# Mixture of experts: dense experts replaced by 23 blocks of 128 gathered rows, weights of all experts on chip

## The reference

```
logits = xt @ router_w.T + router_b            # 8 routed experts
top_vals, top_idx = top_k(softmax(logits), 2)
top_vals = top_vals / sum(top_vals)
h = einsum('td,efd->tef', xt, w_up)            # 256 -> 512
y = einsum('tef,edf->ted', silu(h), w_down)    # 512 -> 256
out = einsum('ted,te->td', y, combine)         # combine is 0 except for two experts
out = out + silu(xt @ shared_w_up.T) @ shared_w_down.T
x = x + out
```

## Time and profile before

| what | value |
|---|---|
| median of 3 runs | 2829.75 us (2828.48 to 2829.79) |
| span of the profiled execution, first to last instruction | 2820.9 us |
| TensorE busy in the span | 2592.8 us (92%) |
| VectorE, ScalarE, GpSimd busy | 1386.3, 1042.5, 532.0 us |
| granted TensorE clock, mean | 0.967 |
| mixture layer, first instruction to the first of the next layer | 998.75 to 1267.14 us |

### The profile page before, as it was taken

The page is one execution under the profiler, slowest core; times in us unless marked ns, Lnnn a source line. Parts: engine busy times, 40 slices in busy tenths (PEclk is TensorE's granted clock), DMA queues, the critical chain, the costliest instruction groups (busy, mean ns, idle before and its releaser), DMA issues. The chain is left out here.

```text
span 2820.9 us, 91874 instructions
## 1 busy us (share of the span) xinstructions
PE 2592.8 (92%) x42047; PEld 1855.1 (66%) x42047; DVE 1386.3 (49%) x2238; ACT 1042.5 (37%) x1400; POOL 532.0 (19%) x400
## 2 busy tenths in 40 slices
PE   7999999999999789998999999999979999988798
PEld 3666666666666556664666666666647777777466
DVE  4454544544544831115545455555465454554378
ACT  2333333333323421114444444444434445444223
POOL 2423424434324000002111111111011111111000
PEclk8999999999998579999999999999999999999899
DMA  2110110110100030101111111112010000000200
GB/s 90 32 43 25 37 37 25 37 37 27 42 20 2 1 121 30 45 20 44 43 33 41 34 40 37 37 37 68 3 51 3 3 3 3 4 3 4 79 1 16
DMA packets 49607, 88.88 MB, mean 32 GB/s; under 512 B 8544, under 2 KB 44224, under 8 KB 47952
## 3 DMA queue, kind: packets, MB, share of 16 engines
q1 hardware_dynamic: 49200, 83.08, 9.6%
q0 software_dynamic: 32, 0.02, 0.0%
HBM read 82.04 MB, written 1.05 MB: 29 GB/s over the span
## 5 line engine op out<-in xcount | busy, mean ns | idle before, releaser
L634 DVE TENSOR_REDUCE x_mx<-banks 128x2 f32<-128x800 f32 (+1 forms) x512 | 505.3, 990 | 162.4 <-PE banks L779 133.2
L804 PE MATMUL banks<-x_wv,x_cT 128*128 128x256 f32 (+1 forms) x1664 | 419.3, 394 | 12.3 <-DVE x_nmb L641 12.3
L709 PE MATMUL banks<-x_cT,x_wk 128*128 128x400 f32 (+1 forms) x1024 | 385.4, 519 | 9.3 <-DMA x_cT<-in_ctx 5.9
L804 PEld LDWEIGHTS banks<-x_wv,x_cT 128*128 128x128 f32 (+1 forms) x1664 | 296.4, 187 | 83.6 <-issue 24.5
L527 ACT ACTIVATE x_PT<-banks 128x2048 f32<-128x2048 f32 (+1 forms) x112 | 196.5, 1755 | 372.1 <-PE banks L839 372.1
L529 ACT ACTIVATE x_PT<-banks,x_kbs 128x1024 f32<-128x1024 f32 (+1 forms) x208 | 221.1, 1110 | 287.7 <-PE banks L839 287.7
L652 DVE COPY x_V<-banks 128x512 f32<-128x512 f32 (+1 forms) x224 | 146.2, 653 | 338.1 <-PE banks L804 337.7
L709 PEld LDWEIGHTS banks<-x_cT,x_wk 128*128 128x128 f32 x1024 | 189.5, 193 | 140.5 <-issue 26.8
L839 PE MATMUL banks<-x_qbd,x_kT 32*128 32x128 f32 x6656 | 248.6, 272 | 0.0
L839 PEld LDWEIGHTS banks<-x_qbd,x_kT 32*128 32x128 f32 x6656 | 244.0, 183 | 3.5
L821 PE MATMUL banks<-x_PT,x_V 128*32 128x64 f32 x13312 | 233.8, 221 | 3.8 <-issue 3.0
(11 more groups left out here) (353 smaller groups left out, 3671.4 us busy)
## 6 DMA issues: line engine op xcount, KB each, us to landing
x_cT<-in_ctx SPq DMA_DIRECT2D x96, 400.0 KB, 3.6
x_cT<-in_ctx SPq DMA_DIRECT2D x32, 401.0 KB, 3.6
e_wu<-in_mo_up SPq DMA_DIRECT2D x9, 512.0 KB, 3.5
e_wd<-in_mo_down SPq DMA_DIRECT2D x9, 512.0 KB, 4.5
x_mrow<-in_mask_row SPq DMA_DIRECT2D x1, 3202.0 KB, 16.2
t_w<-in_db_w SPq DMA_DIRECT2D x3, 1024.0 KB, 7.2
d_wqk<-in_db_qk SPq DMA_DIRECT2D x1, 2048.0 KB, 7.9
t_wgu<-in_fp_gu SPq DMA_DIRECT2D x1, 1536.0 KB, 10.4
```

The source lines that it names most:

```text
L634: dve.reduce_max(mx[:, H0[k]:H0[k] + 3:2, kb], g.PS[:, first:first + 2, 0:KBS[kb]], AXX).then_inc(max_read, 1)
L709: last = pe.matmul(PJ[pb][:, 0:KBS[k]], wk[:, c, gg, :], cT[:, (p + 1) % 2, c, KB0[k]:KB0[k] + KBS[k]], start=c == 0, stop=c == KC - 1)
L804: last = pe.matmul(PJ[pb][0:CHK[c + k], D * k:D * k + D], cT[:, p, cc, 128 * (c + k):128 * (c + k) + CHK[c + k]], wv[:, cc, :], start=cc = ...
```

## The change

The routed experts no longer run on all rows. Each of the 1024 rows chose two experts, so there are 2048 row copies; sorted by expert, with each expert's part filled up to a multiple of 128, they fit in at most 23 blocks of 128 rows (`NBK`), and each block belongs to one expert. The shared expert stays as it was and runs first.

The steps of the new `moe`:

- The weights of all nine experts (`Experts`, 72 KB in each partition) are loaded by SyncE during the latent attention, together with a fill of the DRAM table `rows` (3 MB).
- The layer norm writes into `XE`, rows of 258 values: the 256 normalised ones, the number of the row's place in the output table and its first expert.
- VectorE computes `sel` (the two chosen experts), TensorE counts them with two small matmuls, and VectorE turns the counts into a slot for each copy (`slot_i`) and an owner for each block (`owner_i`).
- GpSimd writes each tile twice into `rows` by indirect DMA, 16 DMAs of 128 rows.
- SyncE waits for all 16, then loads blocks into a ring of four (`xg`). TensorE, for each block: two transposes (`moved`), up with the owner's weights, at an address read by `value_load`, Silu on ScalarE, four transposes (`turned`), down. VectorE copies the result to `y`, GpSimd writes it by indirect DMA to the DRAM table `picks`, 23 DMAs of 128 rows.
- The next layer begins with eight loads of `picks` ahead of its own loads, and VectorE adds both picks of each row with their weights before its layer norm.

The core of the diff, shortened:

```diff
+            pool.wait_ge(ex.filled, 16)
+            for k in (0, 1):
+                pool.wait_ge(slot_done, k + 1)
+                for t in range(NT):
+                    pool.indirect_dma_start(out=ex.rows[:, :], out_offset=bass.IndirectOffsetOnAxis(ap=slot_i[:, k, t:t + 1], axis=0),
+                                            in_=XE[:, t, :], in_offset=None).then_inc(sent, 16)
...
+            sp.wait_ge(sent, 16 * 2 * NT)
+            for i in range(NBK):
+                if i >= XR:
+                    sp.wait_ge(xt_full, i - XR + 1)
+                    sp.wait_ge(y_out, i - XR + 1)
+                sp.dma_start(xg[:, i % XR, :], ex.rows[128 * i:128 * i + 128, :]).then_inc(xg_in[i % XR], 16)
...
+            def moved(i):
+                pe.wait_ge(xg_in[i % XR], 16 * (i // XR + 1))
+                pe.wait_ge(*((xt_out, i - 1) if i >= 2 else (acc, 9 + 5 + i)))
+                for c in range(KC):
+                    last = pe.transpose(g.P[4 + i % 2][:, 128 * c:128 * c + 128], xg[:, i % XR, 128 * c:128 * c + 128], g.ident[:, :])
+                last.then_inc(xt_full, 1)
+            def up(i):
+                pe.wait_ge(xt_out, i + 1)
+                if i >= 2:
+                    pe.wait_ge(bh_out, i - 1)
+                e = pe.value_load(owner_i[0:1, i:i + 1], min_val=0, max_val=NR - 1)
+                for c in range(KC):
+                    last = pe.matmul(g.P[i % 2][:, :], xT[:, i % 2, c, :], ex.up[:, bass.ds(e, 1), c, :].rearrange("p a n -> p (a n)"),
+                                     start=c == 0, stop=c == KC - 1)
+                last.then_inc(bu_full, 1)
+                return e
...
+            for i in range(NBK):
+                if i + 1 < NBK:
+                    owners[i + 1] = up(i + 1)
+                turned(i)
+                if i + 2 < NBK:
+                    moved(i + 2)
+                if i >= 1:
+                    down(i - 1, owners.pop(i - 1))
+            down(NBK - 1, owners.pop(NBK - 1))
...
+            for i in range(NBK):
+                pool.wait_ge(y_out, i + 1)
+                pool.indirect_dma_start(out=mv.flat[:, :], out_offset=bass.IndirectOffsetOnAxis(ap=place_i[:, i % YR:i % YR + 1], axis=0),
+                                        in_=y[:, i % YR, :], in_offset=None).then_inc(mv.placed[i % YR], 16)
...
+            if mask:
+                for r in range(YR):
+                    sp.wait_ge(mk.moved.placed[r], 16 * len(range(r, NBK, YR)))
+                for t in range(NT):
+                    sp.dma_start(picks[:, t, :, :], mk.moved.picks[:, t, :, :]).then_inc(pick_in[t], 16)
...
+            for t in range(NT) if mask else ():
+                dve.wait_ge(pick_in[t], 16)
+                for k in (0, 1):
+                    if k:
+                        dve.wait_ge(pick_done, 2 * t + 1)
+                    dve.scalar_tensor_tensor(g.X[:, t, :], picks[:, t, k, :], mk.moved.weight[:, k, t:t + 1], g.X[:, t, :],
+                                             ALU.mult, ALU.add).then_inc(pick_done, 1)
```

More of the change, by code:

```diff
@@ L9 @@
 U32 = mybir.dt.uint32
+I32 = mybir.dt.int32
 ALU = mybir.AluOpType
@@ L1029, in latent_attention, with _ @@
         block = ctx.enter_context(nc.Block())
+        @block.sync
+        def _(sp):
+            for dst, src, arrived in coming:
+                sp.dma_start(dst, src).then_inc(arrived, 16)
         @block.gpsimd
@@ L1302, in moe @@
         find_in, found, index_done = sem("find_in"), sem("found"), sem("index_done")
[L1304 to L1311 removed]
+        NC = 6
         block = ctx.enter_context(nc.Block())
@@ L1398, in _ @@
+            for j in (0, 1):
+                after(dve.tensor_tensor(eq[:, :, j, :], pick[:, j, :, :], picked[:, :, :], ALU.mult))
+                after(dve.reduce_sum(mv.weight[:, j, :], eq[:, :, j, :], AXX))
             dve.wait_ge(find_in, 48)
-            dve.scalar_tensor_tensor(place[:, :], mk8[:, :], 4096.0, number[:, :], ALU.mult, ALU.add).then_inc(found, 1)
+            dve.scalar_tensor_tensor(number, mk8[:, :], 4096.0, number, ALU.mult, ALU.add).then_inc(found, 1)
             dve.wait_ge(found, 1)
-            dve.tensor_reduce(first[:, 0:1], place[:, :], AXX, ALU.min).then_inc(found, 1)
+            dve.tensor_reduce(first[:, 0:1], number, AXX, ALU.min).then_inc(found, 1)
@@ new lines, in turned, with down @@
+            def turned(i):
+                pe.wait_ge(bh_out, i + 1)
+                if i >= 2:
+                    pe.wait_ge(bt_out, i - 1)
+                for f in range(FC):
+                    last = pe.transpose(g.P[2 + i % 2][:, 128 * f:128 * f + 128], bh[:, i % 2, 128 * f:128 * f + 128], g.ident[:, :])
+                last.then_inc(bt_full, 1)
+            def down(i, e):
+                pe.wait_ge(bt_out, i + 1)
+                pe.wait_ge(*((y_out, i - 1) if i >= 2 else (acc, 9 + 7 + i)))
+                for f in range(FC):
+                    last = pe.matmul(g.P[6 + i % 2][:, 0:D], bhT[:, i % 2, f, :], ex.down[:, bass.ds(e, 1), f, :].rearrange("p a n -> p (a n)"),
+                                     start=f == 0, stop=f == FC - 1)
+                last.then_inc(bd_full, 1)
@@ new lines, in _ @@
+            shared_up(0)
+            pe.wait_ge(c_in, 80)
+            pe.wait_ge(ones_done, 1)
+            pe.wait_ge(sel_done, 1)
+            chosen = sel[:, :, :].rearrange("p t e -> p (t e)")
+            pe.matmul(g.P[4][:, 0:NT * NR], upper[:, :], chosen, start=True, stop=True)
+            pe.matmul(g.P[4][:, NT * NR:2 * NT * NR], ones[:, :], chosen, start=True, stop=True).then_inc(cnt_full, 1)
+            shared_up(1)
+            pe.wait_ge(cnt_out, 1)
+            shared_down(0)
+            shared_down(1)
```

257 lines of the change are left out of this document (178 added, 79 removed).

## The result

The changed kernel takes 2752.05 us (median of 4 runs, 2750.76 to 2753.02) against 2829.77 us (4 runs, 2828.48 to 2829.99) for the kernel before on the same chip. The ratio is 0.9733 (0.9718 to 0.9747): 77.7 us less. The prediction was 2755, range 2722 to 2800.

What follows compares the result with a forecast made beforehand. It took TensorE to bound the kernel, busy 2592.8 of 2820.9 us, and the mixture stage alone. The next stage beginning 85.3 us earlier, less 11 us it pays, gave -74.3 from 2829.75: 2755 us, range 2722 to 2800.

Steps and rivals of the forecast that it cites:

- Routing: Before the blocks: GpSimd can start its scatters 13.6 us after the shared expert's first up product.
- the chain of thirteen instructions: VectorE, from counts to the first set of scatter destinations: thirteen dependent instructions, 4.3 us with 0.5 us of waits.
- Scatters: GpSimd before the blocks: 16 indirect DMAs of 128 rows at 1.5 us each, 24 us, then 1.4 us to land.
- scatters by rows: Rival, GpSimd: an indirect DMA costs by its rows; gain gone at 5.5 us each, 2938 us at 8.2; chance 0.08.
- The first block: First block load: in at 41.3 us after the first up product, TensorE idle for some 11 us before it.
- Pace of the blocks: Mixture: the ring of four block buffers sets 5.2 us a block, bounds 4.3 to 6.4.
- register load on the path: Rival, TensorE in the blocks: its queue drains at each load, a block takes 6.0 to 7.0, 2773 to 2796; chance 0.15.
- Clock in the blocks: TensorE in the blocks: granted clock 1.00, after a start at half clock.
- half clock: Rival, TensorE in the blocks: a block takes 8.4 us, 74 us more in all, 2829 us; chance 0.05.
- End of the mixture: Behind the blocks: last copy, last scatter and barrier add 0.5 + 1.5 + 0.8 us before the next stage.
- Next layer: Next layer's start: loading and adding expert outputs delays root and key evictions, costing 11 us (8 to 16).
- Time around the span: Whole kernel: the 8.9 us between median time and profiled span lie around the span and stay unchanged.

Runs made afterwards that it cites:

- The eight more scatters: Changed kernel plus eight more indirect DMAs of 128 rows to a table nobody reads, waited for before the first block load: 2758.24 us, ratio 0.9771.
- the ring of eight: Changed kernel with eight block buffers instead of four, placed in the shared expert's hidden values: 2729.39 us, ratio 0.9672.
- the late root: Changed kernel with ScalarE taking the next layer's layer norm root after the first key products' evictions instead of before: 2745.8 us, ratio 0.9724.

## Why the prediction was right

**Routing.** First scatter 15.1 us after the first up product; predicted 13.6. The counts came at 9.2 us (predicted 9.0). From there to the scatter are 6.0 us instead of 4.6, and the chain of thirteen instructions is the smaller part of that: it took 4.5 us against the 4.3 of the sum (one of the two large ones 1.07 us instead of 0.69). What was sized too small was what lies around it: 0.6 us from the count matmuls' start to VectorE's first instruction and 0.9 us from the end of its last to GpSimd's first DMA, for which the sum has 0.3 together.

**Scatters.** The largest unknown: 1.27 us each, where I took 1.5, with its lower bound 1.02 for the issue alone. With two longer ones that makes 20.9 us for sixteen instead of 24. The Trainium skill ("DMA: Bandwidth & Descriptors", Anatomy of one DMA — SWDGE (gpsimd) path) says that many descriptors can be emitted before their cost shows, and the traces agree: 128 rows cost GpSimd 0.96 us, 16 rows 0.85 to 1.07. The landing of the output scatters is 2.4 us; an estimate by that section's formula (2.0 us plus 128 KB over 436 GB/s) gives 2.3. The rival "scatters by rows" is dead (its turning point, 5.5 us a scatter, would have been 40 ns per added row and not 45). The first block: 39.75 us, predicted 41.3. The eight more scatters confirm that each counts with about its full pitch, and idle of TensorE before the first block was 9.3 us, predicted 11.

**Pace of the blocks.** Ring of four as the bound: 5.1 us by the working, 5.2 taken, 5.1 measured; the ring of eight shows 4.1 without it. The rival "register load on the path" is dead: the load takes 0.30 us on the queue and is covered, except in the first and the third block, where it costs the 0.8 us that I took. The Trainium skill ("DMA: Bandwidth & Descriptors", Latency and other measured facts) gives a `tensor_load` a floor of about 600 ns; the trace's records of it are 0.30 us, the longest 0.49, and the measurement decides. From the first transposes to the last down product 118.4 us, predicted 122.2: nineteen rounds at 5.1 instead of 5.2 are 2 us of it.

**Clock in the blocks.** 1.00 (1058 to 1171); the rival "half clock" is dead. The first block ran at 0.53, as predicted.

**End of the mixture.** Predicted 0.8 us of barrier behind the last scatter; measured 4.2 (and 6.3 instead of 2.8 from the last down product to the next layer). This is the step that came out wrong: "The last copy, the last scatter and the barrier add 0.5 + 1.5 + 0.8". I took the barrier from the earlier trace rows, where VectorE's 0.83 come at the end of a layer whose only indirect DMA lay 240 us back; behind an indirect DMA just issued GpSimd's drain stands between the layers, and it grows with the DMAs of the layer. 3.5 us, made up for by scatters and blocks: 164.5 us to the next layer where 166.3 were predicted.

**Next layer.** +12.5 us, predicted +11. The mechanism was right (evictions behind the root, the root behind the adds; the late root gives back 6.8 us), the adds ended at 11.1 us (predicted 10.7). The term missed the table load of ScalarE, 1.28 us, which stands between the statistics and the root. It was on ScalarE's path before too. There it followed the mask directly, when the statistics were already there:

```profile
1270.60 0.17 DVE L89 TENSOR_SCALAR ln_rs<-ln_mv 128x8 f32<-128x8 f32 x1
...
1271.33 1.28 ACT L149 ACT_TABLE_LOAD   x1
```

The term counted VectorE's instructions from the last add on and went straight to the root. In the changed kernel the load starts when the statistics are there (1191.32, behind a wait of 9.72). It needn't be so: in the late-root kernel it runs ahead of the wait (1194.07, and then 0.61 us of wait before the root), so part of what that edit gave back can be the load; and the changed kernel's own mixture begins with it, too:

```profile
995.40 1.28 ACT L153 ACT_TABLE_LOAD   x1 [3.10 <-PEq L998]
...
999.06 0.21 ACT L153 ACTIVATE ln_sd<-ln_rs 128x8 f32<-128x8 f32 x1 [2.38 <-DVE ln_rs L93]
```

In the program two waits stand directly before the late one's ACTIVATE, and one before each of the others; that this decides is not tested.

**Time around the span.** I took 8.9 us as lying around the span. The profiled run of the changed kernel took 2750.76 us with a span of 2748.9: 1.9 us. The kernel before, too, takes only 1.7 to 2.8 us more than its span in its runs on other chips, so the profiled execution of before was most likely shorter than the median by some 7 us (its own time is not on record). The sum's difference was made of stages and stays; had the base been the 2820.9 + 1.9 of the profiled execution, 2748.5 us would have come out for the profiled 2750.76.

The sum by steps, predicted and measured: first block 41.3 and 39.75, blocks 122.2 and 118.4, end 2.8 and 6.3, next layer +11 and +12.5: -74.3 and -74.6 us. Four errors of 1.5 to 4 us, two of either sign, cancelled; the agreement to 0.3 us is luck, the agreement of each term to 4 us is not. The rest of the 77.7 us, some 3 us, is placed by no stage; variation between executions is of that size.

## What to carry to other kernels

A chain that passes through a ring of buffers has a pace of its own, the round trip over the number of buffers: work it out beside the engines' busy time, as a deeper ring gave 19 us here at no cost in work. When work moves to the start of the next layer, look at what is queued behind it on each engine: one line of order on ScalarE was worth 6.8 us of that stage. Indirect DMAs were cheap one by one, with 16 rows as with 128 (some 0.96 us on GpSimd), but more than some ten back to back beside TensorE work that mattered were not, and the drain behind them at a layer's end has to be counted.

## What the hardware showed that I had not expected

- Forty indirect DMAs back to back on GpSimd (39 of them with 128 rows) slowed TensorE to one pass in 2.8 us, with the first late product after ten to twelve of them: 31.7 us more from the first up product to the next layer, of which the drain at the end has some 4. Twenty cost 7.1 us there, of which the drain has some 3. One run of each. The cause is open: the DMA engines were at 0.29 and no wait is shown.
- GpSimd's drain at the end of a layer: 2.6 to 2.8 us behind one or two indirect DMAs, 3.5 with 21, 4.5 to 4.6 with 40 and 41, 5.2 with 48.
- A register load from SBUF on TensorE's queue takes 0.30 us and is covered between products, also where their addresses come from the register; where TensorE waits right before it, it costs some 0.8 us.
- ScalarE's table load (1.28 us) stands behind the wait for its ACTIVATE's input in one place (1191.32 in the changed kernel) and ahead of it in others (995.40 there, 1194.07 with the late root). Look up in the timeline which it is.
